# Second GNN layer: the MLP's first product in a bank of its own and a supertile ahead, the fifth tile's weights and the fold in one shared bank, last in TensorE's step

## The reference

```python
h = relu(layernorm(x));  x = x + segment_sum(h[src] * edge_weight[:, None], dst)   # layer 0
h = relu(layernorm(x))                                                               # layer 1
hid = relu(edge_feat @ W1 + b1)                        # 32 -> 64, for every edge
w = (hid @ W2 + b2).reshape(e, 4, 8, 8)                # 256 weights for every edge
# s = h[:, :8], v = h[:, 8:].reshape(n, 8, 3), taken at src; sh0, sh1 = edge_sh
m0 = 0.25 * (einsum(s_e * sh0, w_000) + C110 * einsum(v_e, sh1, w_110))
m1 = 0.25 * (einsum(s_e, sh1, w_011) + einsum(v_e * sh0, w_101))
x = x + segment_sum(concat(m0, m1), dst) + self_interaction(h)
```

## Time and profile before

| what | value |
|---|---|
| median of three runs | 9337.08 us (9321.34 to 9354.07) |
| the profiled execution's own time | 9330.14 us |
| its span, first to last instruction | 9328.3 us |
| TensorE matmul busy | 79% of the span, 46802 matmuls |
| VectorE busy | 58%, 12253 instructions |
| ScalarE, GpSimd busy | 33%, 52% |
| mean granted TensorE clock | 0.856 of 2.4 GHz |

### The profile page before, as it was taken

How to read it: one execution, slowest core, us unless ns; L and a number is a source line. 1 busy time by engine, 2 the same in 40 slices (tenths; PEclk the granted TensorE clock), 3 DMA queues, 4 the chain that set the end, 5 groups by cost and what they waited for, 6 DMA issues and landing times.

```text
span 9328.3 us, 170251 instructions
## 1 busy us (share of the span) xinstructions
PE 7326.0 (79%) x46802; PEld 4946.4 (53%) x46802; DVE 5420.8 (58%) x12253; ACT 3091.8 (33%) x13298; POOL 4880.8 (52%) x5215
## 2 busy tenths in 40 slices
PE   6888888888888886777777777777777777777777
PEld 5777777676777775444444444444444444444444
DVE  6666666666666665555555555555555555555555
ACT  2222222222222222433433343333333433333334
POOL 4666656666666665444444444444444444444444
PEclk9999999999999997788888888888888888888887
DMA  3111111111111111111111111111111111111111
GB/s 81 25 26 25 26 25 26 25 26 25 26 26 26 25 25 26 28 22 23 22 22 23 23 23 22 21 22 22 22 22 23 22 23 22 22 23 22 22 23 23
DMA packets 376870, 235.14 MB, mean 25 GB/s; under 512 B 114825, under 2 KB 373209, under 8 KB 376333
## 3 DMA queue, kind: packets, MB, share of 16 engines
q0 software_dynamic: 163424, 84.00, 6.9%
q1 hardware_dynamic: 212428, 147.61, 6.2%
q10 hardware_dynamic: 990, 3.21, 0.1%
HBM read 229.19 MB, written 5.23 MB: 25 GB/s over the span
## 4 chain that ended last, share of the span: by engine, by line
PE 30%; another core or an unknown queue 26%; issue 18%; DVE 18%; DVEq 5%; ACT 2%; DMA 0%; ACTq 0%; POOL 0%; POOLq 0%; SPq 0%
PE w_ps L696 22%; DVE prod L1174 4%; DVEq L993 3%; DVE t L1179 2%; PE w_ps L706 2%; PE hp_ps L824 2%; PE w_ps L777 2%; DVE z L1211 1%; DVE reduced_sb L1142 1%; DVE acc L1000 1%; DVE reduced_sb L1139 1%; DVE prod L1183 1%; DVE vsh L1158 1%; DVE pick L1010 1%
## 5 line engine op out<-in xcount | busy, mean ns | idle before, releaser
L446 POOL DMA_INDIRECT z<-h_table,idx x5107 | 4836.7, 947 | 4359.1 <-DVE prod L1183 2015.2
L696 PE MATMUL w_ps<-parts,pick 128*128 128x448 f32 x11662 | 2766.0, 390 | 355.2 <-issue 284.1
L696 PEld LDWEIGHTS w_ps<-parts,pick 128*128 128x128 f32 x11662 | 2284.4, 201 | 635.7 <-issue 422.0
L548 ACT ACTIVATE z<-z,squares 128x32 f32<-128x32 f32 x3125 | 798.4, 311 | 2758.1 <-issue 2511.8
L824 PE MATMUL hp_ps<-parts,pick 128*128 128x448 f32 x4340 | 1190.6, 413 | 50.7 <-issue 48.6
L1164 DVE TENSOR_TENSOR p<-w_ps,scalars 128x320 f32<-128x320 f32 x625 | 302.9, 485 | 1498.9 <-remote 1486.7
L824 PEld LDWEIGHTS hp_ps<-parts,pick 128*128 128x128 f32 x4340 | 857.8, 211 | 283.5 <-issue 224.1
L599 ACT ACTIVATE hid<-w_ps,b_sb 128x320 f32<-128x320 f32 x625 | 329.6, 527 | 1946.0 <-remote 1702.7
L777 PE MATMUL w_ps<-w_sb,hid 64*128 64x256 f32 x5000 | 929.9, 497 | 5.2 <-issue 4.3
L1010 DVE TENSOR_TENSOR pick<-sc_ps,feat 128x896 fp32r<-128x896 f32 x833 | 889.7, 1089 | 52.6 <-issue 44.6
L793 PE MATMUL sc_ps<-prod,onehot 128*32 128x344 f32 x5000 | 672.1, 475 | 300.1 <-issue 168.1
(11 more groups left out here) (96 smaller groups left out, 6429.1 us busy)
## 6 DMA issues: line engine op xcount, KB each, us to landing
z<-h_table,idx POOLq DMA_INDIRECT x5107
feat<-key_table SPq DMA_DIRECT2D x311, 192.0 KB
ft_sh_sb<-in_ft_sh SPq DMA_DIRECT2D x625, 90.0 KB
feat<-key_table SPq DMA_DIRECT2D x210, 64.0 KB
h_table<-big SPq DMA_DIRECT2D x10, 280.0 KB
rel_sb<-in_dst_t SPq DMA_DIRECT2D x1, 1562.5 KB
idx_all<-in_src_t SPq DMA_DIRECT2D x1, 1532.5 KB
squares<-in_ew_t SPq DMA_DIRECT2D x1, 1532.5 KB, 12.5
```

The costliest lines, as they stand in the source:

```text
L446: pool.indirect_dma_start(z[:, r, u, :], None, rows, bass.IndirectOffsetOnAxis(ap=idx[:, r, u:u + 1], axis=0)).then_inc(z_in[r], 16)
L548: last = nc.scalar.activation(z[:, r, u, :], z[:, r, u, :], ACT.Copy, scale=ew_all[:, bass.ds(n * G + u, 1)])
L696: mm = pe.matmul(fold_ps[:, pick_banks[k], 0:NC * D], pick[:, k, blk, :], parts[:, t, :, blk, :], start=(blk == 0 and t == 0), stop=(blk = ...
```

## The change

PSUM banks of layer 1 are dealt out anew. `w_ps[:, q, 0:2]` keeps tiles 0 to 3 of the weights, in two sets. Bank (0, 2) holds the fifth tile's weights and the fold, one set for all supertiles. Bank (1, 2) holds both halves of the MLP's first product, one set. Since both halves now lie in one bank, `w1` becomes two 128-row matrices padded with zeros, and each half is a product over all 128 rows; the count of products is unchanged. TensorE issues `hidden` of n+1 in its step n, then the gather, then the weights of four tiles, then the edge sums, then waits for `last_wts_used` and issues the fold and the fifth tile. ScalarE makes `hid` of n+1 in its step n. VectorE splits three operations in two, the fifth tile first, so that `last_wts_used` comes early; `select` moves behind the products. Outside layer 1, `st_inv` takes the place of `st_neg`.

```diff
-        total1_ps = [w_ps[0:D, q, 2, 384:384 + WIN] for q in range(2)]
+        last_wts_ps = w_ps[:, 0, 2, 0:WN].rearrange("p (e c) -> p e c", c=4 * MUL)
+        total1_ps = w_ps[0:D, 0, 2, 384:384 + WIN]
-        hidden_ps = [w_ps[:, q, 1:3, 0:HALF // 2] for q in range(2)]
+        hidden_ps = w_ps[:, 1, 2, 0:HALF].rearrange("p (h e) -> p h e", h=2)
@@ ScalarE, edge_rows
-                if s is None or s < S:
-                    act.wait_ge(hidpre_ready, n + 1)
-                    if s is None or s >= 2:
-                        act.wait_ge(wts_ready, n - 1)
-                    relu_hidden(r % 2).then_inc(hid_ready, 1)
+                if s is None or s + 1 < S:
+                    act.wait_ge(hidpre_ready, n + 2)
+                    if s is None or s >= 1:
+                        act.wait_ge(wts_ready, n)
+                    relu_hidden((r + 1) % 2).then_inc(hid_ready, 1)
@@ TensorE
-                    mm = pe.matmul(hidden_ps[q][:, h], w1_sb[rows, :], ft_sb[rows, r, :], start=True, stop=True)
+                    mm = pe.matmul(hidden_ps[:, h], w1_sb[:, h], ft_sb[:, r, :], start=True, stop=True)
...
-                if s is None or 2 <= s <= S + 1:
-                    pe.wait_ge(wts_used, n - 1)
-                if s is None or s < S:
-                    pe.wait_ge(ft_in[r], (b + 1) * 16)
-                    hidden(r, q).then_inc(hidpre_ready, 1)
+                if s is None or s + 1 < S:
+                    pe.wait_ge(ft_in[(r + 1) % R1], (b + (r + 1) // R1 + 1) * 16)
+                    pe.wait_ge(hid_ready, n + 1)
+                    hidden((r + 1) % R1).then_inc(hidpre_ready, 1)
                 if gathers_half and s != 3:
                     half_gather()
+                if s is None or s < S:
+                    pe.wait_ge(hid_ready, n + 1)
+                    if s is None or s >= 2:
+                        pe.wait_ge(wts_used, n - 1)
+                    weights(q)
                 if s is None or 3 <= s <= S + 2:
                     edge_sums()
-                if s is None or s < S:
-                    pe.wait_ge(hid_ready, n + 1)
+                if s is None or 1 <= s <= S:
+                    pe.wait_ge(last_wts_used, n)
                 if s is None or s >= 4:
                     pe.wait_ge(sum1_reduced, n - 3)
                     pe.wait_ge(tail_copied, n - 3)
-                    total = fold_sums(q, q)
+                    total = fold_sums(q)
                 if s is None or s < S:
-                    weights(q).then_inc(wts_ready, 1)
+                    last_weights(q).then_inc(wts_ready, 1)
@@ VectorE, products: the operations L1164, L1169, L1174 by tiles
+                scalar_products(last_wts_ps, last_tile)
                 dve.wait_ge(coef_ready, n + 1)
+                vector_rows(last_wts_ps, last_tile)
                 take()
                 step(2)
+                scalar_rows(last_wts_ps, last_tile).then_inc(last_wts_used, 1)
+                scalar_products(wts_ps[q], first_tiles).then_inc(prod_step, 1)
+                vector_rows(wts_ps[q], first_tiles)
+                scalar_rows(wts_ps[q], first_tiles).then_inc(wts_used, 1)
+                select()
```

More of the change, by code:

```diff
@@ L139, in gnn_two_layers @@
         st_sum, st_neg, st_var = (sb(n, [NP, J]) for n in ("st_sum", "st_neg", "st_var"))
-        st_std, st_inv = (sb(n, [NP, J]) for n in ("st_std", "st_inv"))
+        st_std, st_inv = sb("st_std", [NP, J]), st_neg
         st_eps = st_var
@@ L165, in gnn_two_layers @@
         one_sb = sb("one_sb", [P, 1])
-        w1_sb = sb("w1_sb", [P, P])
+        w1_sb = sb("w1_sb", [P, 2, P])
         b1_sb = sb("b1_sb", [P, 1])
@@ L598, in relu_hidden @@
             def relu_hidden(q):
-                return nc.scalar.activation(hid[:, q].rearrange("p (h e) -> p h e", h=2), hidden_ps[q], ACT.Relu, bias=b1_sb[:])
+                return nc.scalar.activation(hid[:, q].rearrange("p (h e) -> p h e", h=2), hidden_ps, ACT.Relu, bias=b1_sb[:])
             def scale_rows(n, r, q, selection=lambda: None):
@@ L761, in _, with hidden @@
             self_interaction(GR - 1, GU - 1)
-            def hidden(r, q):
+            def hidden(r):
                 for h in range(2):
-                    rows = slice(h * HID, (h + 1) * HID)
-                    mm = pe.matmul(hidden_ps[q][:, h], w1_sb[rows, :], ft_sb[rows, r, :], start=True, stop=True)
+                    mm = pe.matmul(hidden_ps[:, h], w1_sb[:, h], ft_sb[:, r, :], start=True, stop=True)
                 return mm
             def weights(q):
-                for k, cols in enumerate((2 * WN, 2 * WN, WN)):
+                for k in range(2):
                     rows = slice(32 * k, 32 * k + 3)
-                    pe.matmul(w_ps[:, q, k, 0:cols], ones_sb[rows, :], b2_rows[rows, 0:cols], start=True, stop=False)
+                    pe.matmul(w_ps[:, q, k, :], ones_sb[rows, :], b2_rows[rows, :], start=True, stop=False)
                 for j in range(2):
@@ L776, in weights, with last_weights @@
                         half = slice(k * HID, (k + 1) * HID)
-                        pe.matmul(w_ps[:, q, k, j * WN:(j + 1) * WN], hid[half, q, j * P:(j + 1) * P], w2_sb[half, :],
-                                  start=False, stop=(j == 1))
+                        mm = pe.matmul(w_ps[:, q, k, j * WN:(j + 1) * WN], hid[half, q, j * P:(j + 1) * P], w2_sb[half, :],
+                                       start=False, stop=(j == 1))
+                return mm
+            def last_weights(q):
+                rows = slice(64, 67)
+                pe.matmul(w_ps[:, 0, 2, 0:WN], ones_sb[rows, :], b2_rows[rows, 0:WN], start=True, stop=False)
                 for k in range(2):
                     half = slice(k * HID, (k + 1) * HID)
-                    mm = pe.matmul(w_ps[half, q, 2, 0:WN], hid[half, q, 2 * P:HALF], w2_sb[half, :], start=False, stop=True)
+                    mm = pe.matmul(w_ps[half, 0, 2, 0:WN], hid[half, q, 2 * P:HALF], w2_sb[half, :], start=False, stop=True)
                 return mm
@@ L868, in wide_weights @@
                 pe.nop(nofuse=True)
-                hidden(0, 0).then_inc(hidpre_ready, 1)
+                hidden(0).then_inc(hidpre_ready, 1)
                 pe.wait_ge(hid_ready, n + S + 1)
                 pe.nop(nofuse=True)
-                weights(0).then_inc(wts_ready, 1)
+                weights(0)
+                last_weights(0).then_inc(wts_ready, 1)
             def wide_sums1(turn):
@@ L1163, in products, with scalar_products @@
                 dve.wait_ge(wts_ready, ready)
-                nc.vector.tensor_tensor(p011[:], wts[:, :, 2 * MUL:3 * MUL].rearrange("p (g o) i -> p g o i", g=G),
-                                        scalars[:, q].unsqueeze(2).to_broadcast([P, G, MUL, MUL]), ALU.mult
-                                        ).then_inc(prod_step, 1)
-                select()
+                def scalar_products(wts, tiles):
+                    return nc.vector.tensor_tensor(
+                        p011[:, tiles], wts[:, :, 2 * MUL:3 * MUL].rearrange("p (g o) i -> p g o i", o=MUL),
+                        scalars[:, q, tiles].unsqueeze(2).to_broadcast([P, tiles.stop - tiles.start, MUL, MUL]), ALU.mult)
```

56 lines of the change are left out of this document (33 added, 23 removed).

## The result

The forecast was 9391 us and slower; the kernel became faster. The median after is 8966.44 us (8954.28 to 8978.65, 4 runs) against 9345.58 us before on the same chip: ratio 0.9595, 95% interval [0.9567, 0.9623], 379 us less. The profiled execution took 8962.36 us, 367.8 less than that of before.

The account below looks back on a forecast made before the run. It took TensorE to be paced by its instruction count, about 0.097 us each. To the profiled 9330.14 us it added 61 us for one waiting instruction, all other terms at nothing: 9391 us, range 9225 to 9540.

Parts of the forecast that it names:

- What sets the rate?: TensorE in both layers: paced by its instruction count, about 0.097 us per weight load or matmul, 10 us holds enforcing it.
- the 61 us for one more waiting instruction: TensorE's step: at least one waiting instruction added to some 92, 0.097 us each, 61 us over 625; bounds 0 and 190.
- TensorE's wait for hid: TensorE behind a hold: this wait goes; bounds a gain of 247 us and a loss of 36 us, taken as zero.
- Rival C: TensorE's round trip to ScalarE sets the rate, not the holds: faster, 9252 or 9083 us, range 9120 to 9300; chance 0.24.
- both its marks: Signs of the round-trip rival: p011's "remote" total well below 1335 us, and layer 1's granted clock above 0.82.
- What is late next: TensorE behind a hold: `last_wts_used` comes 0.9 us after `wts_ready`, against 0.72 us now, so one wait replaces the other.
- The hidden product: Over 128 rows in one bank: 0.27 us more, 169 us if TensorE's work were the path; nothing by the pace.
- No row shows two row tiles in one bank: Claim about the profile: the trace cannot say whether row tiles may share a PSUM bank, as the skill denies.
- `select` behind the products: VectorE's `select` moved later: `picked` frees TensorE's bank about 2 us later, hidden unless TensorE gets ahead; priced at nothing.
- VectorE's six operations: Three operations become six: 0.22 us a supertile, 137 us over 625, laid into 3.3 us of waiting; taken as 0.
- Rival D: VectorE's reduce waits for late edge sums: 312 us less 78, 9564 us, range 9460 to 9650; chance 0.16.

Follow-up runs that it names:

- e4: Kernel before with four more tiny products in every step of layer 1: 9354.31 us (ratio 1.0002); on a 6562 us chip 6562.58 us (1.0001).
- e7: Kernel after with the gather products of layer 1 issued twice: 9116.7 us, ratio 0.9748 to the kernel before.
- e1: Kernel after with hidden and its ReLU back in the supertile's own step: 9107.62 us (ratio 0.9724); on a 6562 us chip 6529.91 us (0.9954).
- e3: Kernel before with hidden products over all 128 rows, w1 zero-padded, banks as before: 9346.27 us (ratio 0.9996); on a 6562 us chip 6562.49 us (1.0001).
- e9: Kernel after without GpSimd's gathers in layer 1: 6428.03 us on a 6562 us chip, ratio 0.9793 to the kernel before.
- e10: Kernel before without GpSimd's gathers in layer 1, on 6562 us chips: 6157.73 us (ratio 0.9383), again 6160.51 us (0.9389).
- e2: Kernel after with the four tiles' weights back behind the edge sums: 9194.22 us (ratio 0.9831); on a 6562 us chip 6530.47 us (0.9953).
- e12: Kernel after with hidden, its ReLU and the old order put back, without GpSimd's gathers in layer 1: 6429.36 us on a 6562 us chip, ratio 0.9825.

## Why the prediction was wrong

*The step that failed* is the answer to "What sets the rate?": "TensorE is paced by its count of instructions, about 0.097 us for each weight load or matmul, and the 10 us holds are how the pace is enforced". It came from two rates that lay near each other, 5.00 and 5.16. e4 makes 5.56 of the second at no cost, the change 5.51, e7 6.2. The agreement was chance. The whole amount of the sum over 9330, the 61 us for one more waiting instruction, was a price by this pace; no run adds such an instruction alone, and eight more of TensorE's own cost nothing (e4).

*What stands in its place:* on these chips a completion of TensorE can come up to 10 us late, and what a step costs hangs on which engine waits for it. The prediction had the waits and their sizes. It put TensorE's wait for hid at zero, "since under a pace by count an idle spell is made up by a shorter hold", and VectorE's wait before p011 has no term in the sum at all. That is where the gain lies, but not at face value. Of p011's 1.87 us a supertile 1.28 come back in front of the pick, the reduce and `take`; with 0.36 less before `select` that leaves about 0.93, less 0.34 of more work: the 0.59 us of the step. TensorE's 1.92 us of waiting for hid in e1 are worth 0.24. What delays the signals themselves is open.

*Rival C* had the direction and the sign of both its marks (p011's "remote" well below 1335 us, clock above 0.82). Its size, 78 us and at most 247, was too small: it priced the lead at 78 us net of the hidden product, where the table gives 105 to 129, and missed the order of the step, 205 to 229 us, altogether.

*What is late next* was to be `last_wts_used` at 0.9 us a hold. The terms as written, 0.15 + 384 x 0.00104 + 0.17, add up to 0.72 and not 0.9; in three cases of the timeline after (from 6010.78, 6018.37 and 6026.62), the four operations take 1.03 to 1.23 us. TensorE's fold waits for it 48.3 us in all, 0.09 a supertile. The long holds seldom stand in front of these operations now.

*The hidden product* got longer as predicted, 0.54 to 0.81 us at the full clock (L767 at 6004.92), and it reads 1.43 instead of 0.90 at half. But the 169 us "if TensorE's own work were the path" take the length for the price. The next product starts only 0.07 us later (e3 on both chips, e9), 43 us over 625. e3 has each half in a bank of its own and reads the same 0.81, so the length is that of two 128-row products one behind the other and not of the shared bank.

The Trainium skill, TensorEngine Tiling (Array Packing), section Gotcha 1: PSUM Pressure, says that different row tiles cannot access the same PSUM bank simultaneously. The prediction's "No row shows two row tiles in one bank" is wrong: the fifth tile's weights are such a row. L781 writes `w_ps[half, q, 2, ...]`, two halves of 64 rows into different partitions of one bank, and its four instructions of 256 columns take 0.65 us where four of 160 columns take 0.81 one behind the other. They start in two pairs, 0.27 us from pair to pair and 0.01 us within a pair. So for different partitions of a bank this trace does not agree with the sentence, and the measurement decides; two row tiles in the same partitions of one bank, which a shared bank for hidden would have needed, are in no run.

*`select` behind the products* was called hidden "unless TensorE gets ahead". Where TensorE does get ahead, in e9, the wait for it is there, 0.16 us a supertile. *The bias of the fifth tile* as a product apart had no term; it is 0.21 us there.

*VectorE's six operations* were put at 0.22 us more; the windows say 0.34. They are laid into idle time, which is still 3.03 us, as predicted.

*Rival D* was right on its place and nearly on its size, and wrong on its sum: it moved the idle time and left out what p011 gives back. The reduce waits 149.9 + 108.8 = 258.7 us in 539 supertiles, 0.48 us each, where before it waited 38.9 in 560, 0.07; its price was 312 / 625 = 0.50. The pick, which D names too, waits 0.63 us a supertile more. But the same move that makes the edge sums late brings `wts_ready` out of the long holds, and p011's "remote" wait gives back 1335.3 / 560 - 288.3 / 539 = 1.85 us.

## What to carry to other kernels

Two equal rates are no mechanism: before a pace is made the ground of a forecast, ask what other row would differ if it were true, and carry the plain reading (an engine waits 2.4 us a step for this signal) as a term of its own. Take its face value as an upper bound: here 1.87 us of it went, and the step became 0.59 us shorter. Where completions come late, price an edit by what waits for each of them, and by the next wait in line. Add up busy and idle time of the engine that waits most: the change made VectorE's work longer by 0.34 us and the step shorter by 0.59. And an edit's worth hangs on the path: -4.1% with late signals, +4.4% where TensorE's own work is the path (e9 against e10), and -0.5% for its near relatives e1 and e2 where gathers are.

## What the runs showed of the hardware

The same kernel takes 9345 us on some chips and 6562 on others. On the first, the first hidden product of layer 1 starts at 3730 us (before), on the second at 2975 (e3). On the first, the granted clock of layer 1 is 0.82 and `wts_ready` is 3.7 us late in the mean, 10.8 at most; on the second (e3, e4, e9, e10, e12) it is 1.00 and 0.02 us.

The late ones lie mostly in the stretches at the full clock (2.4 GHz). In the trace of before, from 4000 to 9000 us, 372 of these matmuls end there and 75% of their signals are over 1 us late; 187 end at half (1.2 GHz), and 6% are. After the change it is 70% of 348 and 25% of 190. Of the delays over 6 us before, 93% have the clock's fall to half inside them, while TensorE issues its products with gaps between them (1.10 us ahead of the last one in the earlier trace rows); after, 37%. Which of the two brings the other, or whether a third thing brings both, no run shows.

Three gathers of GpSimd start close to a late one in the mean of before (from 3 us ahead of the matmul's modelled end to 1 us behind it), one close to the others. That is the same time and not yet a cause. What holds the signals is open: no kernel without gathers ran on such a chip.
